# Mixture-of-experts kernel: an expert's rows counted in units of 64, with one block of 384 and one of 320 behind its blocks of 256

## The reference

```python
gate = jnp.einsum('bsd,ed->bse', x, Wg) + routing_bias
_, top_idx = jax.lax.top_k(gate, K)
...
probs = jax.nn.softmax(masked_gate, axis=-1)
weights = probs * mask
out = _swiglu(x, Ws1, Ws2, Ws3)                      # shared expert, all tokens
h1 = jnp.einsum('bsd,ehd->ebsh', x, W1)
h2 = jnp.einsum('bsd,ehd->ebsh', x, W2)
eo = jnp.einsum('ebsh,edh->ebsd', jax.nn.sigmoid(h1) * h1 * h2, W3)
out = out + jnp.einsum('ebsd,bse->bsd', eo, weights)
```

## Time and profile before

| | us |
|---|---|
| median of 3 runs (997.65 to 999.4) | 998.45 |
| span of the profiled execution | 999.4 |
| PE busy | 976.0 |
| DVE, ACT, POOL busy | 564.3, 508.6, 545.6 |
| experts' stage (first product of expert 0 to first product of the late shared blocks) | 716.2 |
| of it PE busy (198 to 914) | 710.69 |

### The profile page before, as it was taken

How to read it: one execution, slowest core, us unless ns; L and a number is a source line. 1 busy time by engine, 2 the same in 40 slices (tenths; PEclk the granted TensorE clock), 3 DMA queues, 4 the chain that set the end, 5 groups by cost and what they waited for, 6 DMA issues and landing times.

```text
span 999.4 us, 25280 instructions
## 1 busy us (share of the span) xinstructions
PE 976.0 (98%) x8054; PEld 798.7 (80%) x8054; DVE 564.3 (56%) x1411; ACT 508.6 (51%) x1250; POOL 545.6 (55%) x513
## 2 busy tenths in 40 slices
PE   9998999999999999999999999999999999999996
PEld 4665666788887888888688878788888887887885
DVE  4998687745544455554554445454455454544686
ACT  3676354354544555454454545454455454554376
POOL 4554027757633348524864017076888880885873
PEclk9999999999999999999999999999999999999999
DMA  6959024364542333352334213218863882785784
GB/s 224 254 134 181 1 60 130 93 180 126 158 112 83 109 91 96 113 148 88 103 94 137 64 39 117 73 48 182 129 102 69 124 130 53 108 129 88 102 159 125
DMA packets 168051, 113.86 MB, mean 114 GB/s; under 512 B 113596, under 2 KB 160191, under 8 KB 166848
## 3 DMA queue, kind: packets, MB, share of 16 engines
q0 software_dynamic: 29808, 58.37, 27.4%
q1 hardware_dynamic: 115888, 33.15, 15.6%
q10 hardware_dynamic: 22304, 21.76, 6.4%
HBM read 47.09 MB, written 43.12 MB: 90 GB/s over the span
## 4 chain that ended last, share of the span: by engine, by line
PE 78%; POOL 7%; DMA 5%; DVE 4%; issue 3%; SPq 1%; ACT 1%; ACTq 0%; DVEq 0%; POOLq 0%
PE psA L1068 49%; PE psB L1099 19%; PE psA L1016 5%; POOL y_sum L754 4%; DMA rows_by_place<-y_rows,place 2%; POOL rows_by_place L690 2%; PE psB L1102 1%; DMA y_sum<-rows_by_place,place 1%; PE psC L1050 1%; PE psA L1099 1%; DMA row_weights_odd<-rows_by_place 1%; DVE g_lo L1500 1%; SPq L516 1%; PE psB L1029 1%; PE psC L1043 1%
## 5 line engine op out<-in xcount | busy, mean ns | idle before, releaser
L869 ACT ACTIVATE sil<-psA 128x256 f32<-128x256 f32 (+1 forms) x456 | 178.4, 398 | 287.4 <-PE psA L1068 259.9
L754 POOL DMA_INDIRECT y_sum<-rows_by_place,place x128 | 199.9, 1562 | 83.1 <-issue 37.7
L1490 DVE SCALAR_TENSOR_TENSOR g<-psA,sil 128x256 f32<-128x256 f32 (+1 forms) x160 | 71.9, 450 | 306.4 <-ACT sil L869 306.2
L1068 PE MATMUL psA<-xb_odd,work 128*128 128x256 f16 x1980 | 221.1, 273 | 0.5 <-issue 0.4
L1099 PE MATMUL psB<-work,g_hi 128*128 128x256 f16 x1260 | 211.6, 273 | 1.6 <-DVE g_lo L1500 1.3
L1068 PEld LDWEIGHTS psA<-xb_odd,work 128*128 128x128 f16 x1980 | 193.3, 98 | 24.1 <-issue 1.8
L1068 PE MATMUL psA<-xb,work 128*128 128x256 f16 x1782 | 199.0, 273 | 3.5 <-issue 1.3
L1068 PEld LDWEIGHTS psA<-xb,work 128*128 128x128 f16 x1782 | 173.5, 98 | 26.0 <-issue 6.1
L1490 DVE SCALAR_TENSOR_TENSOR psC<-psA,sil 128x256 f32<-128x256 f32 (+3 forms) x296 | 133.2, 450 | 79.5 <-ACT sil L869 74.2
L1099 PE MATMUL psB<-work,g_lo 128*128 128x256 f16 x630 | 171.7, 273 | 0.0
L701 POOL DMA_INDIRECT rows_by_place<-y_rows,place x96 | 95.3, 992 | 136.0 <-DMA rows_by_place<-y_rows,place 121.2
(11 more groups left out here) (176 smaller groups left out, 1033.3 us busy)
## 6 DMA issues: line engine op xcount, KB each, us to landing
stage<-wpack POOLq DMA_DIRECT2D x9, 2176.0 KB, 9.5
rows_by_place<-eb ACTq DMA_DIRECT2D x57, 256.0 KB
work<-xT SPq DMA_DIRECT2D x7, 512.0 KB, 6.1
work<-half_beta SPq DMA_DIRECT2D x6, 512.0 KB, 4.3
work<-x_tok POOLq DMA_DIRECT2D x6, 512.0 KB, 6.6
rows_by_place<-eb ACTq DMA_DIRECT2D x6, 384.0 KB
rows_by_place<-zeros SPq DMA_DIRECT2D x1, 2112.0 KB, 13.7
rows_by_place<-y_rows,place POOLq DMA_INDIRECT x128, 2.5
```

Of the source, the lines that this page charges most:

```text
L754: pool.indirect_dma_start(out=y_sum[:, n, :], out_offset=None, in_=xs, in_offset=bass.IndirectOffsetOnAxis(ap=place[:, k, n:n + 1], axis=0 ...
L869: act.activation(sil[r0:r0 + n, c % SLOTS, 0:T], psA[0:n, chunk_bank(c, T), 0:T], ACT.Silu, scale=1.0 / (XS * WS)).then_inc(silu_ready, 1)
L1068: last = pe.matmul(dst, W[:, ws, k, ci, :], xb[slot][:, KD * xs_ + k, 0:T], start=(k == 0 and n == 0), stop=(k == KD - 1 and n == 2))
L1490: dve.scalar_tensor_tensor(gated_rows(g, c, 0, n, T), src, 1.0 / (XS * WS), sil[r0:r0 + n, c % SLOTS, 0:T], ALU.mult, ALU.mult).then_inc(g ...
```

## The change

Rows are counted in units of 64. With U units (at least 4, and rounded up to a multiple of 4 where U is under 12), U mod 4 says how the expert ends: 0, only blocks of 256; 1, a block of 320 in place of the last 256; 2, a block of 384 in place of it; 3, both, in place of the last two 256. An expert always has at least one block of 256, so the condition around the loop goes. The 320 block has a body of its own on each engine (`TM`), behind the one of 384; its buffers are the tail buffers of the other expert of the pair. It loads, sums and stores three groups of 128, of which the last 64 rows are not the block's. Each expert is given one group more in `rows_by_place`, and the pads go up to there. `block_counts` works the new words out.

```diff
 TL = 384
+UNIT = P // 2
+TM = TL - UNIT
...
         def expert_blocks(eng, w, row, run):
-            full, odd, first, group = row
+            (full, wide, short), first, group = row
...
-            with eng.If(odd > 0):
+            with eng.If(wide > 0):
                 run(TL, eng.snap(first + full), None if group is None else eng.snap(group + JB * full), 4 + w)
+            with eng.If(short > 0):
+                run(TM, eng.snap(eng.snap(first + full) + wide),
+                    None if group is None else eng.snap(eng.snap(group + JB * full) + JL * wide), 5 - w)
...
-                J = T // P
+                J = -(-T // P)
...
-                with pe.If_lt(first_of[w][pe.engine], past_of[w][pe.engine]):
...
-                with pe.If_ne(odd_of[w][pe.engine], 0):
+                with pe.If_ne(wide_of[w][pe.engine], 0):
                     past = pe.snap(past_of[w], donate=True, min_val=SA, max_val=SA + NR)
                     ffn_block(w, past, TL, 4 + w, beside=beside)
+                with pe.If_ne(short_of[w][pe.engine], 0):
+                    past = pe.snap(past_of[w], donate=True, min_val=SA, max_val=SA + NR)
+                    wide = pe.snap(wide_of[w], donate=True, min_val=0, max_val=1)
+                    ffn_block(w, pe.snap(past + wide), TM, 5 - w, beside=beside)
...
-                t.add(dve.tensor_scalar(cnt_i[:, 0, :], inc[:, :, NT - 1], 1.0, P - 1.0, ALU.mult, ALU.add))
+                t.add(dve.tensor_scalar(cnt_i[:, 0, :], inc[:, :, NT - 1], 1.0, 2.0 * P - 1.0, ALU.mult, ALU.add))
```

More of the change, by code:

```diff
@@ L364, in build, with units_of @@
         moves_rows = (nc.sync, nc.scalar)
+        def units_of(eng, units):
+            short, wide = eng.snap(units & 1), eng.snap((units >> 1) & 1)
+            return eng.snap(units >> 2), wide, short
         def expert_row(eng, e):
             word = eng.value_load(blocks[0:1, bass.ds(e, 1)], min_val=1, max_val=(NG + 1) * FIELD ** 2 - 1)
-            groups = eng.snap(word & (FIELD - 1), min_val=1, max_val=NT)
+            units = eng.snap(word & (FIELD - 1), min_val=MAIN, max_val=N // UNIT)
             first = eng.snap((word >> FIELD_BITS) & (FIELD - 1), min_val=0, max_val=NR)
             group = eng.snap(word >> (2 * FIELD_BITS), min_val=0, max_val=NG) if eng in moves_rows else None
-            return eng.snap(groups >> 1), eng.snap(groups & 1), first, group
+            return units_of(eng, units), first, group
         def pair_rows(eng, p):
@@ L377, in pair_rows @@
                 return [expert_row(eng, 2 * p + w) for w in range(2)]
-            word = eng.value_load(pairs[0:1, bass.ds(p, 1)], min_val=1, max_val=(NT + 1) * FIELD ** 2 - 1)
+            word = eng.value_load(pairs[0:1, bass.ds(p, 1)], min_val=1, max_val=(N // UNIT + 1) * FIELD ** 2 - 1)
             first = eng.snap(word & (FIELD - 1), min_val=0, max_val=NR)
[L380 to L383, removed]
+            n = [eng.snap((word >> FIELD_BITS) & (FIELD - 1), min_val=MAIN, max_val=N // UNIT),
+                 eng.snap(word >> (2 * FIELD_BITS), min_val=MAIN, max_val=N // UNIT)]
+            rows = [units_of(eng, u) for u in n]
+            full, wide, short = rows[0]
+            return [(rows[0], first, None),
+                    (rows[1], eng.snap(eng.snap(eng.snap(first + full) + wide) + short), None)]
         def early_slot(i):
@@ L399, in rows_from @@
                 return None if group is None else group + JB * n
[L401 to L406, removed]
-            with eng.If(odd > 0):
+            with eng.Fori(0, turns) as i:
+                run(TB, first + 2 * i, rows_from(2 * i), 2 * w)
+                left = eng.snap(full - 2 * i)
+                with eng.If(left > 1):
+                    run(TB, first + (2 * i + 1), rows_from(2 * i + 1), 2 * w + 1)
+            with eng.If(wide > 0):
                 run(TL, eng.snap(first + full), None if group is None else eng.snap(group + JB * full), 4 + w)
+            with eng.If(short > 0):
+                run(TM, eng.snap(eng.snap(first + full) + wide),
+                    None if group is None else eng.snap(eng.snap(group + JB * full) + JL * wide), 5 - w)
         def blocks_until(eng, e):
-            full, odd, first, _ = expert_row(eng, e)
-            return eng.snap(eng.snap(first + full) + odd)
+            (full, wide, short), first, _ = expert_row(eng, e)
+            return eng.snap(eng.snap(eng.snap(first + full) + wide) + short)
         FINISH = [[S1 + q for q in OWN[i]] + list(range(sum(EXTRA[:i]), sum(EXTRA[:i + 1]))) for i in range(S2)]
@@ L1094, in down @@
                         pe.wait_ge(high_doubled, g + 1)
-                    for j in range(T // P):
+                    for j in range(-(-T // P)):
                         o = down_sum(j)
@@ L1135, in read_first @@
                     nc.regs_alu(first, first, SA, ALU.add)
[L1136 to L1140, removed]
+                else:
+                    split_units(0, c - 2)
             def read_second(word, c):
-                n, first, past, odd = groups_of[1], first_of[1], past_of[1], odd_of[1]
+                n, first = units_in[1], first_of[1]
```

89 lines of the change are left out of this document (61 added, 28 removed).

## The result

| | before | after |
|---|---|---|
| median of 4 runs each, us | 998.92 (997.65 to 999.88) | 1017.01 (1015.8 to 1020.46) |
| ratio after to before | | 1.0187, 95% interval 1.016 to 1.0213 |
| span of the profiled execution, us | 999.4 | 1018.7 |
| mean granted TensorE clock of it | 0.998 | 0.989 |

The change makes the kernel 18.1 us slower. The prediction, 993.2 us with a range of 990.5 to 1003.5, is wrong in sign, and the time lies 13.5 us above the range. Its second case, code that is fetched again, is what happened, at more than twice its price.

What follows compares the result with a forecast made beforehand. TensorE, busy 976.0 of 999.4 us, was taken as the bound. Terms -8.96 + 3.2 + 0.2 + 0.3 gave -5.3 us, so 993.2 us from the median of 998.45, range 990.5 to 1003.5.

Steps and rivals of the forecast that it cites:

- second case: TensorE's loop code is fetched again at its returns: +5 to +10 us, middle 1001.2 us; chance 0.40.
- Term 1: Experts' stage: narrower up products in five tail blocks, 320 columns at 135.8 ns each, save 8.96 us.
- Term 2: Starts of 320 tails: ScalarE's silu late, more registers and jumps; +3.2 us, between +1 and +5.
- The 0.8 that expert 5's exit was to give back: Expert 5's end: TensorE no longer jumps over a 384 body, which had cost 0.8 us.
- Term 3: TensorE's jumps over unused tail bodies, expert 1 now passing two: +0.2 us, 0 to 1.4.
- Term 4: Ahead of the first expert: VectorE's longer block_counts table and more pad rows, +0.3 us.
- its cover: TensorE's wait of 1.2 us or more for the first expert's rows hides the table's 0.65 to 1.65 us.
- (e): GpSimd's last gathers and its conversions meeting block ends: taken as 0, conversions -1.5 to +1.5 us.
- No row shows whether nine stay: TensorE's loop with two 320 bodies touches eight packets, one more fetched ahead; whether all stay was left open.
- the 0.53 against 0.40: Chances: 0.53 for the forecast with no code fetched again, 0.40 for code fetched again.
- the rival: TensorE's loop code fetched again, 1.8 to 2.6 us a wait, three or four waits: 998 to 1005 us; chance 0.40.

Runs made afterwards that it cites:

- e1: Kernel before, with two never-run tail bodies, one per weight set, added to TensorE's pair loop: 1026.35 us, ratio 1.0263.
- e2: Kernel before, with one never-run tail body, for weight set 0 alone, added to TensorE's pair loop: 998.51 us, ratio 1.0002.
- e5: Kernel before, with a never-run tail body for weight set 0 and only its gating half for set 1: 996.49 us, ratio 0.9983.
- e6: Kernel before, with e5's never-run code plus unused code ahead of the loop, shifting it into 8 packets: 1030.98 us, ratio 1.0322.
- e3: Changed kernel with TensorE's loop over pairs of experts written out: 1004.92 us, ratio 1.0062 to the kernel before.
- e7: Changed kernel, loop written out, weight set 1 running its 320 block first on all engines: 999.13 us, ratio 1.0003 to the kernel before.

## Why the prediction was wrong, point by point

- **Term 1, -8.96 us: right.** 54, 3 and 5 blocks; a 320 product 136 ns for 135.8; undisturbed blocks 9.0 us less.
- **Term 2, +3.2 us: right for the 320 tails, too small for the rest.** PE's third chunk came 0.7 to 1.0 us late in the five 320 tails, within the 0.3 to 1.1 given, with silu 2.9 to 3.2 us after PE; over before they cost 4.0 us, and 4.0 is what the term had for them (0.9, 0.9, 0.6, 0.9 and 0.7). But the 384 tails of experts 3 and 6, which it left out, were later too, by 1.1 together (0.72 us of PE's standing at 593.84). The 0.8 that expert 5's exit was to give back did not show, since that return missed. Other ways between blocks came to +1.8, most of it the wait for expert 5's rows. So tails +5.0 and ways +1.8, some 7 in place of 3.2, beyond the bound of +5.
- **Term 3, +0.2 us: wrong.** The double jump was priced by a row of a jump whose target was there. Its second half missed: 4.08 us.
- **Term 4, +0.3 us: its cover held.** The table took 2.3 us for 1.3 (DVE, 160.40 to 162.71), and the fourth and fifth shared blocks took 0.6 and 0.2 us longer on PE, but the first expert waits for its rows in any case (1.66 us at 199.90). The 1.75 us by which expert 0 began later is scatter: it began at 198.2 to 199.5 us in five traces with the short table (before, e1, e2, e5, e6) and at 197.6 to 199.9 in seven with the long one.
- **(e), nothing: right for the sum.** Down parts, where the meetings with conversions show, were 4.5 us before and after; over all kernels they scatter from 2.0 to 5.9.
- **The step that failed** is "No row shows whether nine stay", and the 0.53 against 0.40 that were drawn from it: the forecast took the loop's code to stay on PE, and its sum has no term for code. The size of the loop, the eight packets touched and the ninth fetched ahead were worked out as the experiments bear them out. What they showed is that nine do not stay: one body in the loop that never runs costs nothing, two cost 27.4 us (e2, e1), and the pair e5 and e6 puts the limit between eight and nine packets, the one ahead counted. (The Trainium skill, "Runtime: NRT & Kernel Launch", section "Instruction fetch mechanics", gives PE 128 KiB, refilled in blocks of 16 KiB, which makes eight. The pair e5 and e6 agrees. Of what the Trainium skill says there, the trace of before spoke only against the two lines, and I let the one discredit the other.)
- **Its price was mis-sized as well.** 1.8 to 2.6 us a miss, taken from loads of data, was 4.1 to 4.8. Four misses stood PE 15.2 us longer than before. And a cost was left out: behind a stand of 3 to 9 us the clock is at its lower level for a time, 5.6 us in all. So +20.8 us where +5 to +10 was written, and 1017 where the rival said 998 to 1005.

With the forecast's own terms put right (-9.0, +5.0, +1.8) the change without its code would be worth 2 us, by this sum; no run shows that gain.

## What to carry to other kernels

Code in a loop on one engine has a size. On PE here it stayed up to eight packets of 16 KB, those that the loop touches and the one ahead: add them up before adding a body for a special case, and again when anything ahead of the loop moves it. The profile page's row of the instruction queue tells in one look whether a loop is fetched again. A never-taken body is the cheap test of it, since it changes no work. A special body that saves 1.8 us of the bottleneck engine saves only what is left when the engine that feeds it starts late, here about half.

## What the runs showed of the hardware

- A jump of PE whose code is not there lasts 4.5 to 5.1 us at a loop's return and 3.1 to 4.6 us forward (the changed kernel, e1, e3, e6, e7); a forward one with a return behind it stood PE 9.1 to 10.3 us.
- With one packet too many the whole loop comes again, not the one packet: 48 packets for 20, whether the loop is 7.4 packets long (e1) or 6.7 and badly placed (e6).
- PE's stands of 3.35 to 9.24 us in the changed kernel are followed by a stretch at the lower clock, 1.7 to 2.3 us lost in the block behind. So is e1's stand of 3.31 us, which was for rows and not for code (granted clock 0.61 in the 4.4 us behind it, 1.00 in the 3.5 after), and even e7's of 2.69 us; PE's busy time and granted clock of the 4.1 us behind that one and of the next 4.7:

```profile
641.20:645.30 4.10, 4.08 (x19) 0.62 0.36 74
645.30:650.00 4.70, 4.70 (x35) 0.96 0.00 0
```
